# Banded attention on one core: the order of TensorE's products within a step, and where a group's last value products stand

## The chip, the cores and the metric

The kernel runs on one core of one Trainium2 chip. The metric is the device time of one execution in microseconds. Of three runs of the kernel before, the median is 1149.72 us, the lowest 1143.83 us and the highest 1149.92 us.

## The reference

The reference is one decoder-like stack on x of 2 x 1024 x 128 values. Four layers follow one another, each with a layer norm and a residual: full attention over x, a mixture of 64 experts (plus two shared ones), a banded attention with causal window, and the same mixture again. The change touches only the banded attention:

```
q, k, v = heads of (x @ W + b), 16 heads of width 8        # two batches, s = 1024 in the shape used here
valid   = (j <= i) & (j >= i - 32 + 1)
attn    = softmax(where(valid, q @ k.T * 8**-0.5, -inf))
out     = (attn @ v) @ Wo + bo
```

A query sees itself and the 31 keys ahead of it, so of each row of scores only a band is computed: for a tile of 128 queries, 160 keys.

## The kernel before

**Tiling.** `banded_attention` calls `attend_banded` (L534). The 2 batches x 16 heads are cut into 8 groups `n` of 4 heads; each group is walked in 8 steps `s` of 128 keys. The four heads of a group lie in pairs: pair `pr` 0 on partitions 0 to 47, pair 1 on partitions 64 to 111, and `h` picks the head within a pair. I write "step 4.3" for step 3 of group 4.

**One step on TensorE** (`stage`, L706 to L741) issues, in this order:

- the two mask products (L721, whole array, 128 rows by 128 columns, 320 columns of data), one into each bank `st[pr]`. Each first waits for the exponential of the step before on that bank (L720);
- two scores of pair 0 for a later group (`scores`, L658, 48 rows), which wait until VectorE has reduced the tile before them in the bank `sc[0]`. Each later group's maxima are needed before its exponentials, so its scores run four steps ahead;
- the four transposed scores of this group (L728, 51 rows), added onto the mask;
- a slot of side work (`next(beside, None)`);
- two scores of pair 1 (`sc[1]`);
- the value products of the step before (`weigh`, L662; products of 128 rows by 32 columns of the array into the banks `pv`);
- in step 5 the turn of the next group's maxima (`turn_max`), and then a second slot of side work.

After its eighth step the group's last `weigh` follows at once (L741). It waits for the exponentials of step 7.

**The other engines.** ScalarE (L775 to L798) waits for the transposed scores and takes two exponentials a step (L787), the side slots standing behind the first and behind the second; at step 4 and step 7 it copies half of the group's sums out of `pv` (L794) and counts `u_out`. VectorE (L839 to L850) reduces the two banks of scores (L828), with one side slot between the banks and one behind them. GpSimd copies the next values (L612) once `pv_done` shows that the group before has been weighed, and splits the maxima. SyncE loads the stacks.

**Side work.** Groups 0 to 3 are batch 0; beside them runs `second_batch`, the norm and the q, k, v projections of batch 1. Beside groups 4 to 7 runs `first_batch`: output projection tile by tile (`out_by_tiles_tensor`, L1261), norm and routing of batch 0. Each engine has its own generator and takes one piece of it per slot; semaphores tie the pieces together. Two pieces matter below. In `out_by_tiles`, an odd slot on TensorE holds `project(t)` (L1279) and `turn(t + 1)` (L1268), and the next, even one holds `turn_back(t + 1)` (L1275), which waits for `att_ready`, that is for VectorE's `divide(t + 1)` (L1311, L1315), which waits for the turn. `project` waits for ScalarE's copy (L1301), which ScalarE takes behind its first exponential. In `qkv_tensor` (L1620) the third to sixth pieces wait for VectorE's `rest` (L1682), pieces 16 to 19 counted from 0: step 1.0's and step 1.1's.

The mixture's experts (`experts`) follow as a block of their own when the attention's block has ended.

Of the kernel before, what the change touches and what calls it, by code (L numbers as in the profile page):

```python
# [27 lines left out]
TB = S // P  # L28
# [505 lines left out]
def attend_banded(nc, env, tag):  # L534
# [8 lines left out]
    with ExitStack() as ctx:  # L543
# [30 lines left out]
        def score_blocks(s, k, nxt, nxt2):  # L574

            if s < STEPS - AHEAD:
                return [(1, (k + 1) % 3, s + AHEAD)] if nxt else []
            return [(2, (k + 2) % 3, s - (STEPS - AHEAD))] if nxt2 else []

        @block.sync  # L580
# [70 lines left out]
        def _(pe):  # L651
# [10 lines left out]
            def weigh(n, k, s):  # L662

                pe.wait_ge(exp_done, FREE_ST + n * 2 * STEPS + 2 * s + 2)
                if s == 0:
                    pe.wait_ge(u_out, ONE + n * 2)
# [39 lines left out]
            def stage(r, k, nxt, nxt2):  # L706
# [7 lines left out]
                for s in range(STEPS):  # L714
                    width = BAND if s < STEPS - 1 else P
                    if s == STEPS - AHEAD and nxt2:
                        pe.wait_ge(loaded[(k + 2) % 3], (r + (k + 2) // 3) * LOADS + LOADS)
                    for pr in range(2):
                        e = 2 * s + pr
                        pe.wait_ge(exp_done, n * 2 * STEPS + e + 1)  # L720
                        pe.matmul(st[pr][:, :], env.ident16[:, :], mask_k[:, :], start=True, stop=True)  # L721
                    blocks = score_blocks(s, k, nxt, nxt2)
                    for off, kk, qt in blocks:
                        scores(n + off, kk, qt, 0)
# [8 lines left out]
                    next(beside, None)  # L733
                    for off, kk, qt in blocks:
                        scores(n + off, kk, qt, 1)
                    if s:
                        weigh(n, k, s - 1)
                    if s == STEPS - AHEAD + TURN and nxt:
                        turn_max(n + 1)
                    next(beside, None)  # L740
                weigh(n, k, STEPS - 1)  # L741
# [4 lines left out]
        def _(act):  # L746
# [24 lines left out]

            second, first = second_batch(), first_batch()
            copy_max(0)

            def stage(r, k, nxt, nxt2):  # L775
# [4 lines left out]
                for s in range(STEPS):  # L780

                    if s >= 2:
                        act.wait_ge(pv_done, ONE + n * STEPS + s - 1)
# [7 lines left out]
                    if s in (TB // 2, STEPS - 1):  # L791
                        half = 0 if s == TB // 2 else 1
                        act.wait_ge(pv_done, ONE + n * STEPS + TB // 2 * (half + 1))
                        act.copy(env.u[:, bass.ds(n, 1), half * CH:(half + 1) * CH].rearrange("p o c -> p (o c)"),  # L794
                                 pv[half][:, :]).then_inc(u_out, 1)
# [1315 lines left out]
```

## Time and profile before

| | |
|---|---|
| median of 3 runs | 1149.72 us |
| lowest, highest | 1143.83, 1149.92 us |
| span of the profiled execution | 1143.3 us |
| loop of the banded attention, first mask product to the experts' first product | 726.6 to 861.0 us |
| TensorE, VectorE, ScalarE, GpSimd busy over the span | 91%, 81%, 62%, 40% |

The profiled execution has no time of its own beside its span; the span lies 0.5 us under the lowest run, and 6.4 us under the median. A profile lists instructions with start and duration on each engine; a line like L721 is a line of the kernel before. TensorE's products are pipelined: one that lasts 0.23 us may start 0.08 us after the one ahead of it, so for TensorE the starts tell more than the durations. "Idle before" names what the engine had last waited for.

### The profile page before, as it was taken

The page shows a single profiled execution, that of the slowest core. Times are in us where ns is not written, and L with a number is a line of the kernel's source. Part 1 is how long each engine was busy: PE and PEld are TensorE (multiplying, and loading weights), DVE is VectorE, ACT ScalarE, POOL GpSimd, SP SyncE. Part 2 cuts the span into 40 slices and gives each one's busy share as a digit, 9 for nine tenths or more (in the row PEclk, how much of TensorE's full clock was granted, in tenths as well). Part 3 has the DMA queues.
Part 4 walks back from the last instruction along what each step waited for, and adds up shares of the span by engine and source line. Part 5 has one row for each costly group of instructions (what it writes and reads, how often), then busy time and mean ns, then how long its engine had stood idle before and what let it go on. Part 6 is the DMA issues. An engine that isn't in the chain of part 4 may idle for free. (4 is left out here: it accounts for less than half of the span.)

```text
span 1143.3 us, 18866 instructions
## 1 busy us (share of the span) xinstructions
PE 1044.1 (91%) x6314; PEld 427.5 (37%) x6314; DVE 925.3 (81%) x2139; ACT 709.0 (62%) x1089; POOL 461.7 (40%) x434
## 2 busy tenths in 40 slices
PE   5769999999999979999999998888888999999998
PEld 4212222222222325444444443334444444444443
DVE  8688999999998467889788776877876779877775
ACT  2537778777787765666666664355465566666664
POOL 4116336532100105565564554100113556556554
PEclk9758999999999989999999999679999999999999
DMA  6901302311200126566764873142206667687662
GB/s 207 253 2 28 81 9 72 80 53 28 54 2 1 43 59 170 163 170 174 196 181 140 218 193 81 34 110 59 72 4 172 157 152 188 171 208 193 182 189 57
DMA packets 72185, 131.63 MB, mean 115 GB/s; under 512 B 12680, under 2 KB 47624, under 8 KB 72088
## 3 DMA queue, kind: packets, MB, share of 16 engines
q1 hardware_dynamic: 68704, 120.92, 40.5%
q10 hardware_dynamic: 3384, 9.51, 3.1%
q8 instruction: 50, 0.82, 0.3%
q14 instruction: 47, 0.39, 0.1%
HBM read 115.08 MB, written 14.91 MB: 114 GB/s over the span
## 5 line engine op out<-in xcount | busy, mean ns | idle before, releaser
L421 ACT ACTIVATE Aatt_prob<-Aatt_st 128x1024 f32<-128x1024 f32 x256 | 247.7, 1022 | 66.1 <-PE Aatt_st L315 65.1
L487 DVE TENSOR_REDUCE Aatt_mx<-Aatt_sc 128x1 f32<-128x512 f32 x439 | 273.3, 683 | 10.0 <-PE Aatt_sc L302 9.5
L1993 POOL TENSOR_TENSOR M1ex_low<-M1ex_hid,M1ex_high 128x512 f16<-128x512 f32 x132 | 152.8, 1157 | 136.2 <-ACT M1ex_high L1892 70.1
L1993 POOL TENSOR_TENSOR M2ex_low<-M2ex_hid,M2ex_high 128x512 f16<-128x512 f32 x132 | 152.7, 1157 | 130.8 <-PE M2ex_acc L1848 73.3
L302 PE MATMUL Aatt_sc<-ks,qs 48*128 48x512 bf16 x496 | 152.5, 408 | 29.5 <-DVE Aatt_mx L487 11.8
L1886 ACT ACTIVATE M2ex_sil<-M2ex_ring,unscale 128x512 f32<-128x512 f32 x132 | 90.7, 687 | 95.3 <-PE M2ex_ring L1831 95.1
L1886 ACT ACTIVATE M1ex_sil<-M1ex_ring,unscale 128x512 f32<-128x512 f32 x132 | 90.7, 687 | 89.4 <-PE M1ex_ring L1831 88.9
L327 PE MATMUL Aatt_pv<-Aatt_prob,vg 128*32 128x512 f32 x1024 | 137.9, 611 | 0.6 <-ACT Aatt_prob L421 0.6
L1930 DVE SCALAR_TENSOR_TENSOR M2ex_ring<-M2ex_ring,unscale,M2ex_sil 128x512 f32<-128x512 f32 x132 | 100.0, 757 | 42.0 <-ACT M2ex_sil L1886 38.9
L1930 DVE SCALAR_TENSOR_TENSOR M1ex_ring<-M1ex_ring,unscale,M1ex_sil 128x512 f32<-128x512 f32 x132 | 99.9, 757 | 36.2 <-ACT M1ex_sil L1886 32.9
L302 PEld LDWEIGHTS Aatt_sc<-ks,qs 48*128 48x128 bf16 x496 | 35.9, 94 | 201.1 <-DVE Aatt_mx L487 167.7
L315 PE MATMUL Aatt_st<-qs,ks 51*128 51x512 bf16 x512 | 105.2, 387 | 4.0 <-ACT Aatt_prob L421 2.6
L1940 DVE TENSOR_TENSOR M1ex_hid<-M1ex_ring,M1ex_cb 128x512 f32<-128x512 f32 x132 | 91.3, 692 | 16.2 <-DVE M1ex_ring L1930 0.9
L1940 DVE TENSOR_TENSOR M2ex_hid<-M2ex_ring,M2ex_cb 128x512 f32<-128x512 f32 x132 | 91.3, 692 | 15.9 <-DVE M2ex_ring L1930 0.5
L828 DVE CUSTOM_DVE_ANT_0 Batt_sc<-Batt_sc,mask 128x160 f32<-128x160 f32 (+1 forms) x256 | 75.2, 347 | 25.5 <-PE Batt_sc L658 24.1
L1892 ACT CAST M1ex_high<-M1ex_hid 128x512 f16<-128x512 f32 x132 | 80.6, 610 | 17.9 <-DVE M1ex_hid L1940 15.9
L1892 ACT CAST M2ex_high<-M2ex_hid 128x512 f16<-128x512 f32 x132 | 80.5, 610 | 12.1 <-DVE M2ex_hid L1940 10.4
L787 ACT ACTIVATE Batt_prob<-Batt_st 128x320 f32<-128x320 f32 x128 | 51.1, 436 | 55.3 <-PE Batt_st L728 54.9
L1829 PE MATMUL M1ex_ring<-M_xh,M_wt 128*128 128x512 f16 x132 | 50.5, 383 | 11.0 <-DVE M1ex_hid L1940 5.4
L248 POOL CAST Aatt_mparts<-Aatt_m 128x32 bf16<-128x32 f32 x8 | 2.6, 325 | 140.1 <-DVE Aatt_m L500 140.1
L1829 PE MATMUL M2ex_ring<-M_xh,M_wt 128*128 128x512 f16 x132 | 50.4, 382 | 5.7 <-DVE M2ex_hid L1940 3.4
L1848 PE MATMUL M2ex_acc<-M2ex_low,M_wt 128*128 128x512 f16 x132 | 50.3, 381 | 1.0 <-POOL M2ex_low L1993 1.0
(437 smaller groups left out, 1959.5 us busy)
## 6 DMA issues: line engine op xcount, KB each, us to landing
M1ex_cb<-comb SPq DMA_DIRECT2D x130, 256.0 KB, 4.1
M2ex_cb<-comb SPq DMA_DIRECT2D x130, 256.0 KB, 4.2
M_wt<-wsplit SPq DMA_DIRECT2D x132, 192.0 KB, 4.0
wsplit<-split_cut SPq DMA_DIRECT2D x9, 704.0 KB, 4.5
qs<-stack SPq DMA_DIRECT2D x32, 96.0 KB
ks<-stack SPq DMA_DIRECT2D x30, 96.0 KB
split_raw<-in_wg_dram ACTq DMA_DIRECT2D x3, 704.0 KB, 8.5
split_raw<-in_wu_dram ACTq DMA_DIRECT2D x3, 704.0 KB, 12.0
```

The source lines that it names most:

```text
L302: mm = pe.matmul(sc_bank(n, i), queries, ks[k][rows, jp, h * CH:(h + 1) * CH], start=True, stop=kind != "excess")
L315: mm = pe.matmul(st[jp][:, half, :], ks[k][rows, jp, kc * P:(kc + 1) * P], qs[k][rows, jp, qh * CH:(qh + 1) * CH], start=True, stop=True)
L327: mm = pe.matmul(pv[32 * j:32 * j + 32, :], vg[k][:, kc, j, :], prob[(2 * s + j % PAIR) % 4][:, j // PAIR, :], start=kc == 0, stop=kc == T ...
L421: act.activation(prob[e % 4][:, :, :].rearrange("p a c -> p (a c)"), st[pr][:, :, :].rearrange("p a c -> p (a c)"), ACT.Exp, scale=SCALE). ...
L487: ins = dve.tensor_reduce(mx[k][:, m, h:h + 1], scores, AX.X, ALU.max)
L828: ins = dve.tensor_tensor_reduce(scores, scores, mask_q[:, first:BAND], -1.0, -BARRED, ALU.add, ALU.min, accum_out=m1[k][:, j, qt:qt + 1])
L1829: pe.matmul(gate(q)[:, :], wt[k][:, 0, :], env.xh[:, cs], start=True, stop=False)
L1886: act.activation(sil[q % 2][:, :], gate(q)[:, :], ACT.Silu, scale=env.unscale[:, 0:1]).then_inc(sil_ready, 1)
L1892: act.copy(high[q % 3][:, :], hid[q % 3][:, :]).then_inc(high_ready, 1)
L1930: dve.scalar_tensor_tensor(up(q)[:, :], up(q)[:, :], env.unscale[:, 1:2], sil[q % 2][:, :], ALU.mult, ALU.mult).then_inc(up_ready, 1)
L1940: dve.tensor_tensor(hid[q % 3][:, :], up(q)[:, :], cb[k][:, c * CH:(c + 1) * CH], ALU.mult).then_inc(hid_ready, 1)
L1993: pool.tensor_tensor(low[q % 3][:, :], hid[q % 3][:, :], high[q % 3][:, :], ALU.subtract).then_inc(low_ready, 1)
```

## The change

Within a step, TensorE's work is put in the order of its tiling: whole-array products first (the side slots and the masks), then all 64-row products (transposed scores, then both pairs' scores), then the 32-column value products. The two side slots move: the slot that stood last in a step now stands ahead of the next step's first mask product (the same place in the stream), and the slot that stood behind the transposed scores now stands between the two mask products. The first slot of groups 0 and 4 is left out on TensorE, which keeps the numbering of the slots against ScalarE and VectorE. Scores of pair 0 no longer stand ahead of the transposed scores.

Between groups of one batch (`carried`), the last `weigh` of a group moves behind the first transposed scores and scores of the next group. ScalarE's copy of the second half of the sums moves behind the two exponentials of the next group's step 0, and the waits on `u_out` are split by half.

```diff
+        def carried(n):
+            return n % G < G - 1
@@ TensorE, weigh
-                if s == 0:
-                    pe.wait_ge(u_out, ONE + n * 2)
+                if s == 0 and n:
+                    pe.wait_ge(u_out, ONE + 2 * n - 1)
+                if s == 3:
+                    pe.wait_ge(u_out, ONE + 2 * n)
@@ TensorE, stage
                     for pr in range(2):
+                        if pr or s or n % G:
+                            next(beside, None)
                         e = 2 * s + pr
                         pe.wait_ge(exp_done, n * 2 * STEPS + e + 1)
                         pe.matmul(st[pr][:, :], env.ident16[:, :], mask_k[:, :], start=True, stop=True)
-                    blocks = score_blocks(s, k, nxt, nxt2)
-                    for off, kk, qt in blocks:
-                        scores(n + off, kk, qt, 0)
                     for h in range(2):
                         for pr in range(2):
 ...
-                    next(beside, None)
-                    for off, kk, qt in blocks:
-                        scores(n + off, kk, qt, 1)
+                    for off, kk, qt in score_blocks(s, k, nxt, nxt2):
+                        for pr in range(2):
+                            scores(n + off, kk, qt, pr)
                     if s:
                         weigh(n, k, s - 1)
+                    elif n and carried(n - 1):
+                        weigh(n - 1, (k + 2) % 3, STEPS - 1)
                     if s == STEPS - AHEAD + TURN and nxt:
                         turn_max(n + 1)
-                    next(beside, None)
-                weigh(n, k, STEPS - 1)
+                if not carried(n):
+                    weigh(n, k, STEPS - 1)
@@ ScalarE, stage
-                    if s >= 2:
+                    if s:
                         act.wait_ge(pv_done, ONE + n * STEPS + s - 1)
 ...
-                    if s in (TB // 2, STEPS - 1):
-                        half = 0 if s == TB // 2 else 1
-                        act.wait_ge(pv_done, ONE + n * STEPS + TB // 2 * (half + 1))
-                        act.copy(...).then_inc(u_out, 1)
+                    if s == 0 and n and carried(n - 1):
+                        sums_out(n - 1, 1)
+                    if s == TB // 2:
+                        sums_out(n, 0)
+                    if s == STEPS - 1 and not carried(n):
+                        sums_out(n, 1)
```

`sums_out(n, half)` is the wait and the copy that stood there before. No product, exponential or reduction is added or dropped.

## Rows read from the trace of the kernel before

**Rows 1.** The page: span, and TensorE's granted clock in 40 slices, tenths of full.
```profile
span 1143.3 us, 18866 instructions
PEclk9758999999999989999999999679999999999999
```

**Rows 2.** Busy time by stretch: us, each engine's busy us, PEclk, DMA share, GB/s.
```profile
726.60:738.30 11.70, 11.18 (x110) 5.07 (x109) 10.61 (x73) 4.81 (x13) 2.55 (x5) 0.54 0.18 46
738.30:756.60 18.30, 16.25 (x142) 7.98 (x143) 14.88 (x67) 11.44 (x25) 0.40 (x1) 1.00 0.27 68
756.60:772.80 16.20, 15.05 (x158) 6.28 (x154) 9.72 (x65) 7.42 (x19) 1.30 (x5) 0.58 0.49 125
...
794.00:816.60 22.60, 21.11 (x220) 12.84 (x221) 18.32 (x95) 10.00 (x29) 1.31 (x5) 1.00 0.33 96
```

**Rows 3.** Timeline of TensorE, step 3.6, no side work: start us, length us, what.
```profile
789.35 0.64 PE L721 MATMUL Batt_st<-mask,ident 128*128 128x320 bf16 x2
789.92 0.24 PE L658 MATMUL Batt_sc<-ks,qs 48*128 48x160 bf16 x1
...
790.14 0.23 PE L728 MATMUL Batt_st<-qs,ks 51*128 51x160 bf16 x1
...
790.96 0.31 PE L721 MATMUL Batt_st<-mask,ident 128*128 128x320 bf16 x1 [0.17 <-ACT Batt_prob L787]
```

**Rows 4.** Timeline of ScalarE in that same step.
```profile
790.47 0.77 ACT L787 ACTIVATE Batt_prob<-Batt_st 128x320 f32<-128x320 f32 x2 [0.70 <-PE Batt_st L728]
```

**Rows 5.** Timeline of TensorE, step 7.5, which has no scores.
```profile
853.15 0.64 PE L721 MATMUL Batt_st<-mask,ident 128*128 128x320 bf16 x2 [0.17 <-ACT Batt_prob L787]
...
854.62 0.64 PE L721 MATMUL Batt_st<-mask,ident 128*128 128x320 bf16 x2 [0.18 <-ACT Batt_prob L787]
```

**Rows 6.** Timeline of TensorE from step 2.7 to step 3.1, over a group's end.
```profile
777.49 0.64 PE L721 MATMUL Batt_st<-mask,ident 128*128 128x320 bf16 x2 [0.17 <-ACT Batt_prob L787]
...
779.40 0.43 PE L671 MATMUL Batt_pv<-Batt_prob,vg 128*32 128x128 f32 x8 [0.50 <-ACT Batt_prob L787]
...
781.11 0.64 PE L721 MATMUL Batt_st<-mask,ident 128*128 128x320 bf16 x2 [0.52 <-ACT Batt_prob L787]
```

**Rows 7.** Timeline of TensorE, step 0.2, at half clock.
```profile
730.53 0.71 PE L721 MATMUL Batt_st<-mask,ident 128*128 128x320 bf16 x2
...
732.52 0.45 PE L721 MATMUL Batt_st<-mask,ident 128*128 128x320 bf16 x1
```

**Rows 8.** Timeline of TensorE beside the output projection: turn 1, step 4.5, turn 7.
```profile
797.67 0.60 PE L1268 MATMUL Batt_side<-ident,u 128*128 128x128 f32 x4
...
806.05 0.60 PE L1268 MATMUL Batt_side<-ident,u 128*128 128x128 f32 x4
806.49 0.43 PE L721 MATMUL Batt_st<-mask,ident 128*128 128x320 bf16 x2
...
806.95 0.36 PE L728 MATMUL Batt_st<-qs,ks 51*128 51x160 bf16 x3
807.40 0.33 PE L1275 MATMUL Batt_side<-ident,Batto_att 128*128 128x128 f32 x1
...
808.68 0.60 PE L1268 MATMUL Batt_side<-ident,u 128*128 128x128 f32 x4
...
813.85 0.60 PE L1268 MATMUL Batt_side<-ident,u 128*128 128x128 f32 x4
```

**Rows 9.** Timeline of ScalarE in step 4.5.
```profile
807.40 0.44 ACT L787 ACTIVATE Batt_prob<-Batt_st 128x320 f32<-128x320 f32 x1 [0.95 <-PE Batt_st L728]
807.77 0.27 ACT L1301 COPY Batto_attT<-Batt_side 128x128 f32<-128x128 f32 x1
```

**Rows 10.** Timeline of VectorE in step 4.5.
```profile
807.05 0.29 DVE L1315 TENSOR_TENSOR Batto_att<-Batt_side,Batto_rden 128x128 f32<-128x128 f32 x1
```

**Rows 11.** Timeline of TensorE, step 1.1, beside the projections.
```profile
749.38 1.16 PE L1634 MATMUL Batt_side<-b_wv,Battqln_xnT 128*128 128x128 f32 x8 [0.35 <-DVE Battqkv_rest L1682]
```

**Rows 12.** Timeline of VectorE in step 1.1.
```profile
750.37 0.74 DVE L1682 SCALAR_TENSOR_TENSOR Battqkv_rest<-Batt_side,b_bqk,Battqkv_part 128x512 f32<-128x512 f32 x1
```

More of the change, by code:

```diff
@@ L770, in first_batch, with sums_out @@
                 yield from route_scalar(act, env, n1, q1, bank, 0)
+            def sums_out(n, half):
+                act.wait_ge(pv_done, ONE + n * STEPS + TB // 2 * (half + 1))
+                act.copy(env.u[:, bass.ds(n, 1), half * CH:(half + 1) * CH].rearrange("p o c -> p (o c)"),
+                         pv[half][:, :]).then_inc(u_out, 1)
             second, first = second_batch(), first_batch()
@@ L790, in stage @@
                             next(beside, None)
-                    if s in (TB // 2, STEPS - 1):
-                        half = 0 if s == TB // 2 else 1
-                        act.wait_ge(pv_done, ONE + n * STEPS + TB // 2 * (half + 1))
-                        act.copy(env.u[:, bass.ds(n, 1), half * CH:(half + 1) * CH].rearrange("p o c -> p (o c)"),
-                                 pv[half][:, :]).then_inc(u_out, 1)
+                    if s == 0 and n and carried(n - 1):
[4 more added lines that the diff above has]
+                        sums_out(n, 1)
                     if s == STEPS - AHEAD + TURN and nxt:
```

## The prediction, made before the changed kernel ran

> **What bounds the kernel now.** I first took the page for the span and the clock [rows 1], then cut the banded loop into stretches [rows 2], then read single steps in the timeline of TensorE and set those of ScalarE and VectorE beside them. The loop fills 726.6 to 861.0 us, 134.4 us for 64 steps, mean 2.1 us; everything else in the program is untouched and follows it in series, so what the loop gains or loses the span gains or loses. The busy shares mislead here: TensorE is busy 16.3 of 18.3 us in the stretch with the projections [rows 2], yet what sets a step differs by kind of step.
>
> *Steps without side work at full clock.* A ring of two engines. Step 3.6 starts its first mask at 789.35 and step 3.7 at 790.96, 1.61 us later, and that mask had waited for an exponential [rows 3]. Round the ring: second mask (0.64 - 0.31 = 0.33 after the first, so 789.68) to the first 64-row product at 789.92 is 0.24; the last transposed product starts 0.22 later at 790.14 and lasts 0.23; the exponentials start at 790.47 and take 0.77 together [rows 3, 4]; then the next second mask. Sum 0.24 + 0.22 + 0.23 + 0.10 + 0.77 + 0.05 = 1.61. VectorE is not in this ring.
>
> *Steps at half clock.* The granted clock reads 0.54 and 0.58 in two stretches, that is mostly 1.2 GHz [rows 2]; 13 steps lie there, and one takes 1.99 us [rows 7].
>
> *Steps beside the output projection* (4.1 to 5.0). TensorE and a chain through VectorE and ScalarE. One period, turn to turn, is 808.68 - 806.05 = 2.63 us [rows 8].
>
> *Steps beside the projections* (0.7 to 1.4). VectorE, with 14.9 busy of 18.3 us [rows 2]; TensorE stood 0.35 us for VectorE's `rest` before the even slot of step 1.1 [rows 11].
>
> **The change part by part.**
>
> *Transposed scores first.* Pair 0's scores leave the ring. The trace shows what the ring is without them: from step 7.5 to 7.6, where no scores remain, 854.62 - 853.15 = 1.47 us [rows 5], against 1.61 [rows 3]: 0.14 a step. The scores then run beside the exponentials, where TensorE had 0.17 us idle before the mask [rows 3]. VectorE gets them some 0.15 us later; it has room where no side work runs. Steps of this kind: 8 clean ones in groups 2 and 3, and six in groups 5 and 6 where VectorE also carries side work, counted at half: 8 x 0.14 + 6 x 0.07 = 1.5 us. Bounds 0 and 14 x 0.14 = 2.0. At half clock TensorE itself nearly fills the step, for the first mask came without a wait [rows 7]; I take 0.07, half the above, for 13 steps: 0.9 us, bounds 0 and 13 x 0.28 = 3.6 (the full-clock gap doubled). Together 2.4.
>
> *Last value products carried over.* At a group's end `weigh` stands 0.50 us for the exponentials, and the next step's second one is short because both masks are free. Two steps over the end of group 2 take 781.11 - 777.49 = 3.62 us against 2 x 1.61 = 3.22 in the middle of a group [rows 3, 6]: 0.40 us a boundary. Once carried, the products lie beside the exponentials. ScalarE's copy of 0.58 us moves into step 0 of the next group, behind the exponentials; ScalarE waits 0.70 us for TensorE in a step [rows 4], so it is covered; were it not, it would cost what is over. GpSimd's copy of the next values comes one step later and is wanted only a group later; nothing else is queued there but the splitting of maxima, which waits for VectorE. There are six carried boundaries; two of them (0 to 1, 4 to 5) lie in the chains below. Four times 0.40, with 0.2 more for the one at half clock: 1.8 us; bounds 0.8 and 2.4.
>
> *Fewer changes of tiling.* A side slot behind the transposed scores cuts the 64-row products in two. In step 4.5 the last of these starts at 806.95 + 0.36 - 0.23 = 807.08 and the side product at 807.40; in an unbroken run they follow each other every 0.07 us ((0.36 - 0.23) / 2). Some of the 0.32 is waiting for VectorE, which ended at 807.34 [rows 8, 10], so the change of tiling itself is bounded by 0.24 us from above and by 0 from below; I take 0.09, twice a step. Further, pair 0's and pair 1's products run side by side when nothing stands between, and two of the six start places fall away: 0.15. Together 0.3 us in a step with side work in its even slot and no chain. Those are 5.7, 6.1 and 7.6: 0.9 us.
>
> The Trainium skill ("TensorEngine Tiling (Array Packing)", section Tiling Modes) says that a change of tiling mode, not of tile, drains the engine. The rows do not separate a drain from a wait here. By that rule alone, with the bound of 0.24 us from the rows for each and 16 steps losing two changes, the loop would win 7.7 us; this is a rival below.
>
> *The even slot between the masks: the output projection.* Here the cover goes. Before, `turn_back` came 0.3 us behind the last transposed product: the masks and the 64-row products (806.49 to 807.31) hid VectorE's `divide`. Now only one mask stands between `turn` and `turn_back`. From the last turn's start (806.05 + 0.60 - 0.27 = 806.38) to `turn_back`'s start at 807.40 is 1.02 us, and VectorE ended 0.06 before it [rows 8, 10]; those 1.02 us are latency and remain. Behind the waiting `turn_back` stand the second mask, the transposed scores, and so the exponentials. Then: `turn_back` to second mask 0.17 (half of its 0.33), to the transposed scores 0.24, their second start and length 0.31, to the exponential 0.09: it starts at 1.83. ScalarE's copy starts 0.37 behind it and takes 0.27 [rows 9], so `project` may start at 2.51, and from `project` to the last turn is 0.60. Period 3.11 us against 2.63. TensorE's own work would have let `project` start at about 2.15, so the copy is late by a further 0.36; both waits are in the 3.11. The six periods from turn 1 to turn 7 took 813.85 - 797.67 = 16.2 us before [rows 8]; now 6 x 3.11 = 18.7: +2.5. The step after turn 7 pays another 0.6 and the boundary gives 0.3 back: +2.8 us in all, bounds +1.0 (if only the first wait bit) and +4.5.
>
> *The same slot beside the projections.* The `rest` that lets a piece go is taken by VectorE behind the first bank of that step's scores. These now stand behind the even slot, which holds TensorE for 1.1 us or more (1.16 for the values [rows 11]). So the odd piece's `rest` comes about as much later. In step 1.0 about half of that had been lost before in other work; in step 1.1 piece 18 stands for `rest` (0.74 us [rows 12]) and piece 19's `rest` can't begin before it is through. Worked through by these durations step 1.1 starts 0.8 us later and step 1.2 starts 2.2 us later, the gain at the boundary 0 to 1 included. VectorE is the bound up to step 1.4, so nothing of it comes back: +2.2 us, bounds 0 and +3.6.
>
> *Sum.* -2.4 - 1.8 - 0.9 + 2.8 + 2.2 = -0.1 us. Against the profiled execution, 1143.3 us becomes 1143.2 us. The median of the runs lies 6.4 us above that span, and I leave that distance as it is: 1149.7 - 0.1, rounded to 1149.6 us.
>
> **The rivals.**
>
> *A. The waits are covered and the drains count.* If VectorE and ScalarE run ahead in the side chains, the losses vanish, and every one of 16 steps with even side work wins 0.3: -2.4 - 1.8 - 16 x 0.3 = -9.0, time 1140.7 us. For it: TensorE is the busiest engine in the loop. Against it: the 1.02 us of latency stand in the rows. The rule of the skill in its strongest form comes to -2.4 - 1.8 - 7.7 = -11.9, 1137.8 us.
>
> *B. The clock.* The two half-clock stretches end sooner because steps are denser. A step takes 1.99 at half and 1.61 at full clock [rows 3, 7]: 13 x 0.38 = 4.9 us, time 1144.7 us. For it: the work per time rises. Against: TensorE was busy 11.2 of 11.7 us there and stayed at half [rows 2].
>
> *C. Slower.* The idle time that the even slot now opens in steps 4.1 to 5.0, some 1.2 us of a period of 3.11, lets TensorE's granted clock fall there to half. Per step the 0.38 above and as much again for the side products: 8 x 0.8 = +6.4, time 1156.0 us. It decides from the point where the stage's clock, 1.00 before [rows 2], falls below about 0.6. Against it: the ring steps at 1.61 us have as large a share of waiting and keep the full clock.
>
> *D. It doesn't do what it says.* The array runs the two pairs in its own order and the transposed scores come no sooner: the 2.4 and 0.9 go, +5.0 - 1.8 = +3.2, time 1152.9 us. Against it: rows 5.
>
> **How the numbers follow.** Chances: forecast 0.48, A 0.19, B 0.10, C 0.13, D 0.10. A measurement of this kernel tells apart about 0.5%, 5.7 us. A lies beyond that, B just inside; of the forecast, with unknowns of some 4 us both ways, a tenth falls out on each side. Faster 0.19 + 0.03 + 0.05 = 0.27; slower 0.13 + 0.01 + 0.05 = 0.19; same 0.54. The forecast's own range is 1144 to 1155; with half of A and C it is 1141 to 1156.
>
> **What would show it.** In the changed profile: ring steps in groups 2 and 3 at 1.47 us (transposed first); no 0.5 us wait before the 128-column value products except after groups 3 and 7 (carried); turn to turn 3.1 us in group 4, with TensorE's L1275 waiting some 0.8 us each for `att` and `project` some 0.3 us for `attT`; step 1.2 starting 2 us later after step 0.7 than before. The prediction is wrong if turn to turn stays near 2.6, or if the clock row of the loop differs from the one before by more than a slice.

## The result, and the profile after

The changed kernel took 1154.81 us, the median of 20 runs, against 1149.70 us for the kernel before, the median of 20 runs on the same chip: a ratio of 1.0054, 95% interval 1.0033 to 1.0076. Ratios, means and half-clock times here and below leave out runs more than 1.5% above the fastest of their kernel; medians are of all runs. The forecast was 1149.6 us, a change of -0.1 us, with "same" as the likeliest case. The time lies just inside the range given, at its upper end, which is no merit of the sum: the median rose by 5.1 us where almost nothing was forecast.

The profiled execution took 1152.56 us with a span of 1150.8 us, 7.5 us more than the span before [rows 1]. The page of the changed kernel, its span and its clock row:

```profile
span 1150.8 us, 18881 instructions
...
PEclk9758999999999989999999998689969999999999
```

The clock row shows the first surprise: besides the 6 and 8 of slices 26 and 27, where 6 and 7 stood before [rows 1], there is a second 6 in slice 30, about 834 to 863 us. A piece of the loop that ran at full clock before now runs at half, from 833.3 to 853.8 us. ("Half clock" is a granted clock of 0.50, the lower of the two levels.)

The loop, from its first mask to the experts' first product, is the stretch 726.6 to 861.0 us before and 726.8 to 870.4 us after. Each row is: stretch, us, busy us of TensorE, its weight loads, VectorE, ScalarE and GpSimd, the granted clock, DMA share, GB/s. Before:

```profile
726.60:861.00 134.40, 116.62 (x1296) 57.07 (x1295) 100.52 (x561) 70.67 (x177) 15.52 (x39) 0.91 0.22 59
```

After:

```profile
726.80:870.40 143.60, 120.00 (x1296) 58.90 (x1296) 98.86 (x561) 70.00 (x177) 15.57 (x39) 0.85 0.20 55
```

The same numbers of instructions take 9.2 us longer; the rest of the program is 1.7 us shorter (behind the loop it has one stretch of 3.4 us at half clock where the kernel before has two), which leaves the 7.5 us. Now the same view cut at the same steps. Before, steps 1.2 to 3.7, 4.0 to 5.0, 5.1 to 5.7, and 6.0 to 6.7 are the stretches from 752.2, 794.1, 816.6 and 831.3 us; the last three:

```profile
794.10:816.60 22.50, 21.05 (x220) 12.75 (x221) 18.32 (x95) 10.00 (x29) 1.31 (x5) 1.00 0.33 96
816.60:831.30 14.70, 12.06 (x154) 5.83 (x152) 12.92 (x87) 6.80 (x17) 2.50 (x5) 1.00 0.17 40
831.30:846.10 14.80, 12.79 (x157) 6.50 (x153) 11.73 (x60) 9.34 (x23) 3.66 (x7) 1.00 0.01 3
```

After, steps 1.2 to 3.7 and those three:

```profile
754.50:794.00 39.50, 35.03 (x434) 16.28 (x432) 28.61 (x180) 20.95 (x53) 3.94 (x15) 0.87 0.34 88
794.00:820.50 26.50, 19.40 (x219) 11.38 (x220) 17.01 (x93) 8.88 (x29) 1.20 (x5) 1.00 0.30 88
820.50:835.70 15.20, 12.31 (x145) 6.03 (x144) 13.04 (x89) 7.16 (x18) 2.62 (x6) 0.92 0.10 23
835.70:855.00 19.30, 18.62 (x156) 9.18 (x153) 12.75 (x67) 9.46 (x23) 3.66 (x7) 0.53 0.01 3
```

| stretch | before, us | after, us | difference | forecast |
|---|---|---|---|---|
| steps 0.0 to 1.1 | 25.6 | 27.7 | +2.1 | +1.8 |
| steps 1.2 to 3.7 | 41.9 | 39.5 | -2.4 | about -2.6 |
| steps 4.0 to 5.0 | 22.5 | 26.5 | +4.0 | +2.8 |
| steps 5.1 to 5.7 | 14.7 | 15.2 | +0.5 | steps 5.1 to 7.7: |
| steps 6.0 to 6.7 | 14.8 | 19.3 | +4.5 | about -2.1 |
| steps 7.0 to 7.7 | 14.9 | 15.4 | +0.5 | |

The forecast column spreads the terms of the sum over their steps. The first two rows came out near the forecast, the second of them in part by the clock, as is shown below; the rest did not.

*The ring, as forecast.* TensorE in the changed kernel, the masks of steps 2.5, 2.6 and (behind them) 2.7:

```profile
775.19 0.64 PE L730 MATMUL Batt_st<-mask,ident 128*128 128x320 bf16 x2
775.76 0.31 PE L735 MATMUL Batt_st<-qs,ks 51*128 51x160 bf16 x4
775.91 0.42 PE L662 MATMUL Batt_sc<-ks,qs 48*128 48x160 bf16 x4
...
776.76 0.53 PE L730 MATMUL Batt_st<-mask,ident 128*128 128x320 bf16 x2
```

The transposed products (L735) lead, the scores (L662) follow 0.15 us behind. Step 2.5 takes 776.76 - 775.19 = 1.57 us and step 2.6 takes 778.18 - 776.76 = 1.42, mean 1.50, where 1.61 stood before [rows 3] and 1.47 was forecast. Not every such step is shorter: step 3.3 went from 1.70 to 2.21 us, because the mask of step 3.4 waits for a stack that is being loaded, a wait that the kernel before does not have:

```profile
786.82 0.45 PE L730 MATMUL Batt_st<-mask,ident 128*128 128x320 bf16 x2 [0.67 <-DMA ks<-stack]
```

*The boundary, half given back.* TensorE over the end of group 2, to be set beside rows 6:

```profile
778.18 0.58 PE L730 MATMUL Batt_st<-mask,ident 128*128 128x320 bf16 x2
...
779.24 0.48 PE L677 MATMUL Batt_pv<-Batt_prob,vg 128*32 128x160 f32 x8
...
780.39 0.45 PE L730 MATMUL Batt_st<-mask,ident 128*128 128x320 bf16 x2 [0.67 <-DMA qs<-Batt_mt]
...
781.15 0.42 PE L677 MATMUL Batt_pv<-Batt_prob,vg 128*32 128x128 f32 x8
...
781.61 0.31 PE L730 MATMUL Batt_st<-mask,ident 128*128 128x320 bf16 x1
```

The 128-column value products of the old group (781.15) stand behind the new group's first scores and no longer wait 0.50 us for exponentials: the carrying over does what it says. But the new group's first mask waits 0.67 us for something that was never late before: the group's maxima, which a transfer brings into the query rows (`qs<-Batt_mt`, issued at 777.31). From step 2.7 to step 3.1 is 781.61 - 778.18 = 3.43 us, against 3.62 before [rows 6] and 2 x 1.47 = 2.94 forecast.

*Beside the output projection, as forecast.* TensorE in step 4.5, to be set beside rows 8:

```profile
808.07 0.60 PE L1284 MATMUL Batt_side<-ident,u 128*128 128x128 f32 x4
808.50 0.30 PE L730 MATMUL Batt_st<-mask,ident 128*128 128x320 bf16 x1
809.41 0.33 PE L1291 MATMUL Batt_side<-ident,Batto_att 128*128 128x128 f32 x1 [0.61 <-DVE Batto_att L1331]
809.58 0.30 PE L730 MATMUL Batt_st<-mask,ident 128*128 128x320 bf16 x1
809.81 0.31 PE L735 MATMUL Batt_st<-qs,ks 51*128 51x160 bf16 x4
...
811.19 0.60 PE L1284 MATMUL Batt_side<-ident,u 128*128 128x128 f32 x4
```

One mask stands between `turn` (L1284) and `turn_back` (L1291), which waits 0.61 us for VectorE; the second mask and all 64-row products stand behind it. Turn to turn is 811.19 - 808.07 = 3.12 us; 3.11 was forecast. ScalarE, in the same step, stands 1.71 us for the transposed scores, against 0.95 before [rows 9]:

```profile
810.22 0.44 ACT L802 ACTIVATE Batt_prob<-Batt_st 128x320 f32<-128x320 f32 x1 [1.71 <-PE Batt_st L735]
```

What TensorE waited for in the whole stretch 794.0 to 820.5 us of the changed kernel (what waits, for whom, us in total, times, longest), of which the kernel before had 0.7 us once and 0.2 us once:

```profile
PE Batt_side L1291 <- DVE Batto_att L1331: 5.2, 8, 1.1
PE Batt_side L1295 <- ACT Batto_attT L1317: 1.5, 7, 0.3
```

### The profile page after: what moved, and what is told of

Same layout as the page of the kernel before. It is cut to its first block and busy times, and to the rows that moved or that the text cites. A ratio compares the mean times of both kernels' runs of the same rounds, so it can differ in the third digit from the quotient of the medians.

```text
span 1150.8 us, 18881 instructions
## 1 busy us (share of the span) xinstructions
PE 1046.9 (91%) x6314; PEld 429.4 (37%) x6314; DVE 923.2 (80%) x2139; ACT 709.1 (62%) x1089; POOL 462.2 (40%) x434
## 5 line engine op out<-in xcount | busy, mean ns | idle before, releaser
L2009 POOL TENSOR_TENSOR M1ex_low<-M1ex_hid,M1ex_high 128x512 f16<-128x512 f32 x132 | 152.9, 1158 | 136.1 <-ACT M1ex_high L1908 70.1
```

What stands on the lines that cost most here:

```text
L2009: pool.tensor_tensor(low[q % 3][:, :], hid[q % 3][:, :], high[q % 3][:, :], ALU.subtract).then_inc(low_ready, 1)
```

## The experiments

The rival theories at this point: W, the added time is waiting that the new place of the even slot causes, to be had back by moving the slot; C, it is the half-clock time that the changed kernel has more of. (The expectations use these letters, and others that they explain.) Runs of one kernel scatter (the changed one: 1152.3 to 1165.0 us), and each run lists its mean granted clock, from which twice the missing share times the run's time is the time spent at half clock. Over all runs here, time rises by 0.28 us for each us of it, within a kernel. So each result below has three numbers: the median with the ratio to the kernel before, the mean time with the mean half-clock time, and the mean moved by that slope to 119 us of half clock, called the levelled time. The kernel before, over its 96 runs: mean 1149.7, half clock 129.0, levelled 1146.9 (error 0.2). The changed one: 1155.8, 142.8, 1149.1 (error 0.35). The runs below were taken in three sittings, each on a chip of its own, and the kernel before differed between them: mean 1147.9 with 123.0 us of half clock beside the first four experiments, 1149.6 with 128.9 beside the four with the slot behind scores or a mask twice, 1151.9 with 136.1 beside the order alone and the three with ring masks. A difference of a few us of half clock between kernels of different sittings therefore shows nothing. The levelled time leans on the slope, and a later section says where that fails.

**The last value products alone.** The kernel before, with only the carrying over (the waits and the place of `weigh`; ScalarE's copy moves as in the change):

```
-                if s == 0:
-                    pe.wait_ge(u_out, ONE + n * 2)
+                if s == 0 and n:
+                    pe.wait_ge(u_out, ONE + 2 * n - 1)
+                if s == 3:
+                    pe.wait_ge(u_out, ONE + 2 * n)
...
+                    elif n and carried(n - 1):
+                        weigh(n - 1, (k + 2) % 3, STEPS - 1)
```

> The kernel before with one part of the change alone: the last value products of groups 0, 1, 2, 4, 5 and 6, and the copy of their second half, move into the next group's step 0; the order within a step is as before. Theory W (waits at the even side slot between the masks cost the time): this part wins what I forecast for it, 0.4 us at each of five or six boundaries, so 1.8 to 2.4 us, ratio to before 0.998. Rival K (carrying the products over costs, because ScalarE's copy or GpSimd's copy of the next values comes late): 2 us or more slower, ratio 1.002 or above. Rival C (only the granted clock of the loop decides): time by its half-clock stretches, no step changed but those at the boundaries.

Measured: 1152.6 us, ratio 1.0027 (0.9996 to 1.0058); mean 1151.2 with 141.0 us of half clock, levelled 1145.1 (error 0.7), which is 1.8 below the kernel before; 1.8 was forecast. The plain ratio, 0.998 expected, is above 1 instead: the kernel has 18 us more of half clock than the kernel before in its sitting. Its TensorE over the end of group 2, at full clock:

```profile
777.76 0.64 PE L727 MATMUL Batt_st<-mask,ident 128*128 128x320 bf16 x2 [0.17 <-ACT Batt_prob L801]
...
779.65 0.45 PE L727 MATMUL Batt_st<-mask,ident 128*128 128x320 bf16 x2 [0.48 <-ACT Batt_prob L801]
...
781.01 0.64 PE L727 MATMUL Batt_st<-mask,ident 128*128 128x320 bf16 x2 [0.16 <-ACT Batt_prob L801]
```

Two steps take 781.01 - 777.76 = 3.25 us against 3.62 [rows 6]: 0.37 gained, 0.40 forecast, and nobody waits for the maxima. So at this boundary the wait of 0.67 us comes from the two parts together: with the transposed scores first as well, TensorE reaches the boundary sooner than the transfer lands. (The order alone, below, waits 0.44 and 0.75 us for the maxima at the ends of groups 1 and 3, and not here.)

**The even slot back behind the transposed scores.** The changed kernel with the slot between masks moved (here and below, conditions that are always true or false are left out of the code shown):

```
                     for pr in range(2):
-                        if pr or s or n % G:
+                        if not pr and (s or n % G):
                             next(beside, None)
...
+                    next(beside, None)
                     for off, kk, qt in score_blocks(s, k, nxt, nxt2):
```

> The changed kernel with the even side slot put back behind the transposed scores (before the scores of both pairs) in all groups; everything else as changed. Theory W: the losses of the changed kernel vanish (4.0 us in steps 4.0 to 5.0, 2.2 in 0.0 to 1.1, some 5 in 5.7 to 6.7) and the gains stay: 4 to 6 us faster than before, ratio 0.995 to 0.997; turn to turn in group 4 back to 2.6 us. Rival C (the order itself thins TensorE's work so that the clock falls to half in groups 5 and 6, wherever the slot stands): that stretch of 20 us remains, ratio 1.000 or above.

Measured: 1149.23 us, 1.0018 (0.9998 to 1.0039); mean 1149.5 with 130.3, levelled 1146.3. A gain of 4 to 6 us on the kernel before was expected; it did not come. Turn to turn was 2.6 us again, so the group 4 loss is the slot's. But steps 1.0 and 1.1 stayed at 4.45 and 5.13 us (before 3.17 and 4.16; changed 4.73 and 5.40). VectorE and TensorE of this kernel in step 1.0:

```profile
747.28 0.33 DVE L846 CUSTOM_DVE_ANT_0 Batt_sc<-Batt_sc,mask 128x160 f32<-128x160 f32 x1 [1.52 <-PE Batt_sc L662]
```

```profile
745.90 1.10 PE L1646 MATMUL Batt_side<-Battqln_xnT,b_wqk 128*128 128x512 f32 x2
...
748.70 1.10 PE L1646 MATMUL Batt_side<-Battqln_xnT,b_wqk 128*128 128x512 f32 x2 [1.10 <-DVE Battqkv_rest L1700]
```

VectorE stands 1.52 us for scores that are queued behind the projection product at 745.90, and then TensorE stands 1.10 us for VectorE's `rest`. The two wait for each other in turn. It is not enough that the slot leaves the masks; it has to be behind the scores.

**The slot back in group 4 only, and from step 5.1 on only.**

```
-                        if pr or s or n % G:
+                        if (pr and not (n in (4, 5) and n * STEPS + s <= 5 * STEPS)) or (not pr and (s or n % G)):
...
+                    if n in (4, 5) and n * STEPS + s <= 5 * STEPS:
+                        next(beside, None)
```

> The changed kernel with the even side slot behind the transposed scores only from step 4.0 to step 5.0 (the output projection). Theory W: turn to turn 2.6 us there, 4.0 us less than the changed kernel, ratio to before 1.002; the half-clock stretch of groups 5 and 6 stays. Rival C: if the half-clock stretch follows from the thin steps of group 4, it goes as well, and the ratio is 0.997.

Measured: 1151.14 us, 1.0020 (0.9997 to 1.0043); 1150.3 with 134.8, levelled 1145.8: 3.3 less than the changed kernel, where 2.5 to 2.8 was the forecast's price of that chain and +4.0 is what the stretch showed. Steps 4.5 to 4.7 take 2.63, 2.59 and 2.60 us again. Its profiled execution also speaks on the clock:

```profile
PEclk8758999999998999999999998688979999999999
...
790.00:816.00 26.00, 24.04 (x216) 13.11 (x213) 16.28 (x90) 10.24 (x29) 1.30 (x5) 0.74 0.11 33
```

The half-clock stretch in group 6 is still there (17.1 us from 835.2, the 7 in slice 30), although group 4 has its old slots; and 13.7 us of half clock now lie in group 4 itself, from 797.7. So, as far as one execution shows it, the stretch in group 6 does not need the waits of group 4.

The second kernel has `n * STEPS + s > 5 * STEPS` in both places:

> The changed kernel with the even side slot behind the transposed scores only from step 5.1 on (norm and routing). Theory W with the clock as its consequence: without the waits of steps 5.7 to 6.2 the half-clock stretch does not come, 4 to 6 us less than the changed kernel, ratio to before 1.000 to 1.002. Rival C (the fall to half clock does not depend on the slot here): the stretch stays, at most 2 us less, ratio 1.004.

Measured: 1152.83 us, 1.0039 (1.0018 to 1.0061); 1152.5 with 131.4, levelled 1149.0. That is the changed kernel's 1149.1: by this measure the place of the slot costs and brings nothing from step 5.1 on, though the mean time is 3.3 us lower, with 11 us less of half clock. Of the 4 to 6 us expected, 3.3 came, and only together with the clock: in its profiled execution 6.8 us of half clock are left in group 6, where the changed kernel has 20.5.

**The slot behind both scores**, ahead of the value products, in all groups:

```
                     for off, kk, qt in score_blocks(s, k, nxt, nxt2):
                         for pr in range(2):
                             scores(n + off, kk, qt, pr)
+                    next(beside, None)
```

> The changed kernel with the even side slot behind the scores of both pairs and ahead of the value products, in all groups. Theory W, second half (in groups 0 and 1 the loss comes from the scores standing behind the slot, not from the slot standing between the masks): steps 1.0 and 1.1, 4.45 and 5.13 us with the slot behind the transposed scores and 4.73 and 5.40 in the changed kernel, return to 3.2 and 4.2 us; at equal half-clock time 2 us less than with the slot behind the transposed scores and 4.5 to 5 us less than the changed kernel, so some 2.5 us faster than before. Rival S (VectorE is bound there for another reason, the later start of the scores within the step): they stay above 4.2 and 4.9. Half-clock time, which by the runs so far costs 0.28 us for each us: between that of before (mean 124 us) and of the changed kernel (143), so the plain ratio lies between 0.998 and 1.003.

Measured: 1146.06 us, 0.9973 (0.9943 to 1.0002); 1147.0 with 137.5, levelled 1141.8, that is 7.3 below the changed kernel and 5.1 below the one before. TensorE of this kernel in a step of group 4:

```profile
803.72 0.43 PE L730 MATMUL Batt_st<-mask,ident 128*128 128x320 bf16 x2
...
804.63 0.33 PE L1293 MATMUL Batt_side<-ident,Batto_att 128*128 128x128 f32 x1
...
805.66 0.60 PE L1286 MATMUL Batt_side<-ident,u 128*128 128x128 f32 x4
806.10 0.43 PE L730 MATMUL Batt_st<-mask,ident 128*128 128x320 bf16 x2
```

No row of the step has a wait, and it takes 806.10 - 803.72 = 2.38 us, against 2.63 before [rows 8] and 3.12 in the changed kernel. Steps 1.0 and 1.1 take 3.21 and 4.24 us, as in the kernel before.

**The same in groups 0 and 1 only**, the slot elsewhere as in the changed kernel (condition `n < 2`):

> The changed kernel with the even side slot behind both pairs' scores in groups 0 and 1 alone (the projections). Theory W: steps 1.0 and 1.1 take 3.2 and 4.2 us, 2.2 to 2.8 us less than the changed kernel at equal half-clock time; groups 4 to 7 keep turn to turn at 3.12 us. Rival S: they stay above 4.2 and 4.9 us and the time at equal half-clock time is that of the changed kernel.

Measured: 1153.55 us, 1.0027 (0.9995 to 1.0059); 1153.6 with 142.3, levelled 1147.0: 2.1 less than the changed kernel at the same half-clock time, so here the slope plays no part. The forecast's term for this chain was +2.2. Steps 1.0 and 1.1: 3.21 and 4.25 us.

**The order alone**, without the carrying over (`carried` returns False and the old wait stands):

> The changed kernel without the carrying over: each group's last value products and the copy of its second half stand where they stood before; the order within the step is the changed one. Theory W: at equal half-clock time 1.9 us more than the changed kernel and 4.2 us more than before (the waits of groups 1 and 4, 5.4 us, less about 1 us for the earlier transposed scores). Whether the carrying over is what adds half-clock time is open (that part alone had a mean of 148 us of it, before 128, the changed kernel 143): if so, this kernel has 125 to 130 us and a plain ratio of 1.004; if it is the order, 140 us or more and a ratio of 1.006 to 1.008.

Measured: 1158.79 us, 1.0046 (1.0016 to 1.0076); 1158.3 with 143.6, levelled 1151.4: 2.3 above the changed kernel, which gives the carrying over its price a second time, and 4.5 above the kernel before. At full clock the price shows at the ends of groups 4 and 6 (step 4.7 takes 3.79 us against 3.15 in the changed kernel, step 6.7 2.13 against 1.84), and not at the end of group 2 (3.34 us for steps 2.7 and 3.0 against 3.43), where the changed kernel waits for the maxima. Which part brings the half-clock time is not settled: against the kernel before in the same sitting the carrying over alone has 18 us more (error 5.5), this kernel 7.5 (error 5), and both parts with the slot behind the transposed scores 7 (error 3).

**More work for TensorE.** If the granted clock follows how densely TensorE works (theory G in the expectations), products that do nothing new, put where it waits, should cut the half-clock time. Pair 0's mask is written twice in every step, which leaves the result as it was; in the changed kernel, and in the one with the slot behind both scores:

```
-                        pe.matmul(st[pr][:, :], env.ident16[:, :], mask_k[:, :], start=True, stop=True)
+                        for _ in range(2 - pr):
+                            pe.matmul(st[pr][:, :], env.ident16[:, :], mask_k[:, :], start=True, stop=True)
```

> The changed kernel with each step's first mask product made twice into the same bank. Between the masks of the changed kernel TensorE waits in the side steps (0.9 us each in group 4), so the extra product is covered there too. Theory G: the half-clock stretch of some 20 us in groups 5 and 6 becomes rare, half-clock time falls from 143 to 125 us or less, and the plain ratio to before falls from 1.0054 to 1.002 or less. Rival N: the half-clock time stays at 140 us and the ratio rises to 1.006 by the added products.

Measured: 1152.36 us, 1.0006 (0.9983 to 1.0028); 1152.0 with 112.7 us of half clock, where the changed kernel has 142.8.

> As the kernel with the slot behind both pairs' scores, and each step's first mask product is made twice into the same bank. In steps without side work TensorE has idle time between its two masks, so the extra 0.14 us costs nothing there; in some 20 steps in which TensorE is full it costs 0.14 to 0.27 us, 3 to 4 us in all. Theory G (the granted clock follows how much TensorE does, and the changed kernel's plain time suffers from more half-clock time): half-clock time falls below that of before, to 110 us or less, which is worth 5 us or more against the changed kernel's 143; plain ratio to before 0.998 to 1.002. Rival N (half-clock time is chance or has another cause): it stays between 125 and 145 us and the ratio is 1.003 or more.

Measured: 1147.54 us, 0.9963 (0.9932 to 0.9994); 1147.1 with 114.1, from 137.5. In both the half-clock time falls by 23 to 30 us, while the mean time falls by 3.8 us in the first and not at all in the second: in steps without a wait ahead of the masks the added product costs its 0.13 us.

**The second mask only in the ring steps**, where the mask stands waiting anyway: `range(2 if pr == 0 and ring(n, s) else 1)`, with `ring` true in steps 1.2 to 3.7, 5.1 to 5.7 and 6.2 to 7.7. In the changed kernel, in the one before, and with the slot behind both scores:

> The changed kernel with the first mask product made twice, but only in steps 1.2 to 3.7, 5.1 to 5.7 and 6.2 to 7.7, where TensorE waits for the exponentials between its masks; the steps beside the projections and the output projection, and those of group 0, are as changed. Theory G (the granted clock follows TensorE's work per time): half-clock time falls from 143 to 125 us or less with at most 1 us of added work, so the plain ratio to before falls from 1.0054 to 1.000 to 1.003. Rival N (the earlier fall in half-clock time came from group 0, where masks twice ended its half-clock stretch 3.4 us sooner): half-clock time stays above 135 us, ratio 1.005.

Measured: 1153.44 us, 1.0014 (0.9981 to 1.0047); 1153.6 with 119.2. The half-clock stretch of 20.5 us in group 6 is down to 3.4 in the profiled execution, from 836.3 us, most of which lies in this row:

```profile
837.00:852.00 15.00, 13.73 (x167) 7.43 (x164) 11.28 (x65) 9.02 (x23) 2.90 (x7) 0.91 0.01 2
```

Steps 6.0 and 6.1 take 2.08 and 2.10 us here, 3.67 and 3.61 in the changed kernel at half clock, 2.20 and 2.55 in the kernel before.

> The kernel before with the first mask product made twice in the same steps (1.2 to 3.7, 5.1 to 5.7, 6.2 to 7.7). Theory G: half-clock time, 128 us on average before, falls to 120 us or less; at 0.28 us for each that is 2 to 3 us faster, ratio 0.998, and fewer runs above 1155 us. If the added product is not covered in the order of before, it costs 0.14 us in some 35 steps, up to 5 us, and the ratio is 1.002.

Measured: 1148.76 us, 0.9957 (0.9931 to 0.9984); 1148.7 with 118.7. This kernel and the last have the same half-clock time and differ by the change alone: 4.9 us by their means. Their profiles differ by stretch, in the order of the table above, by +2.1, -1.2, +4.0, +0.8, about 0 and +0.6 us, together +6.2 where the means say 4.9.

> The slot behind both pairs' scores, with the first mask product made twice in the same steps. Mechanically 5 us less than before (as measured at equal half-clock time for the slot behind the scores), at most 1 us for the added products; half-clock time 120 us or less by theory G instead of 137. Expected 1140 to 1143 us, ratio to before 0.993 to 0.996, the fastest of all. Rival N: half-clock time stays at 137 us, ratio 0.998.

Measured: 1143.87 us, ratio 0.9911 (0.9875 to 0.9947); 1144.0 with 110.5. It beats the changed kernel and the one before. Its page and its loop:

```profile
span 1142.6 us, 18967 instructions
...
PEclk9758999999999999999999999599999999999999
```

```profile
726.80:860.20 133.40, 117.64 (x1342) 58.92 (x1342) 103.19 (x583) 70.85 (x176) 15.58 (x39) 0.92 0.22 60
```

The doubled masks add TensorE work (117.64 us busy, 116.62 before) and next to no time to the ring: steps 3.0 and 7.0, which have no wait to hide them, take 0.13 us more. The waits for transfers are still in it, and longer: the masks wait 4.7 us in all, five times, three for the maxima and two for a stack (1.23 and 1.53 us). The kernel before has none. One of them, at the end of group 2:

```profile
782.33 0.58 PE L734 MATMUL Batt_st<-mask,ident 128*128 128x320 bf16 x3 [0.56 <-DMA qs<-Batt_mt]
```

## Why the prediction was wrong, step by step

The -0.1 us was a small difference of larger terms. The pair with ring masks, at equal clock, shows +6.2 us in its profiles. The step that failed is the gains, which were mis-sized: steps 1.2 to 3.7 gave -1.2 us where -2.6 was forecast, and steps 5.1 to 7.7 gave +1.2 where -2.1 was forecast (transposed scores first in groups 5 and 6 and at half clock, fewer changes of tiling, two carried boundaries). Together that is 4.7 us. The loss beside the output projection was mis-sized by a further 1.2 us (+4.0 for +2.8). And the sum had no term for the clock. Term by term:

*Transposed scores first, full clock (-1.5).* Mechanism right, and the size too in steps 2.5 and 2.6: 1.50 us a step, 1.47 forecast. Over a whole group it brought less, since TensorE now also runs ahead of transfers: steps 3.0 to 3.6 take 10.71 us against 11.21 before, half of the forecast 0.14 a step, with the wait of 0.67 us for the stack in them; the kernel with the order alone, which has no such wait there, takes 10.09. The six steps counted at half in groups 5 and 6 are the mis-sized part, and the pair with ring masks shows them at equal clock (kernel before first): steps 5.2, 5.4 and 5.5 take 1.66, 1.52 and 1.61 us, then 1.88, 1.69 and 1.60, while step 5.3 falls from 2.19 to 1.82, so that steps 5.1 to 5.5 are 0.1 us shorter in all; steps 6.4, 6.5 and 6.6 take 1.41, 1.47 and 1.47 us in both. The latter stood at the ring without scores all along: group 6 has no later group left to score in them, which the trace before would have told. In group 5, where VectorE carries side work, its scores are probably what comes late; whether the 0.15 us by which they stand further back is the whole of it was not measured.

*The same at half clock (-0.9).* Failed. Steps 0.2 to 0.4, at half clock, take 1.99, 2.06 and 1.92 us before, 1.99, 2.00 and 1.93 after. TensorE fills such a step [rows 7], and its products in another order are not fewer.

*Carrying over (-1.8).* Right by itself: -1.8 levelled, 0.37 us at the boundary that was looked at. Only half right in company: the boundary of the changed kernel has 0.19 us less than before, for the mask then waits for the maxima's transfer. The prediction named what moves behind the exponentials on ScalarE and GpSimd, and left out who else must be ready for the new group's first step.

*Fewer changes of tiling (-0.9).* Seen in the steps, not in the sum. At full clock step 6.1 went from 2.55 to 2.10 us and step 7.6 from 2.25 to 2.07 (changed kernel: 1.93), where 0.3 each was forecast; step 5.7 can't be read, since part of it lies in half clock. But the neighbours took it back: 6.2 and 6.3 are longer by 0.24 and 0.28, 7.3 by 0.28, 7.7 by 0.42. From step 5.1 to the end the pair shows +1.2 us where about -2.1 was forecast, and the kernel that puts the slot of these groups back is as fast as the changed one (levelled 1149.0 and 1149.1). A step that ends sooner only meets VectorE's chain sooner. The stronger rule, that a change of tiling mode drains the engine (the Trainium skill, "TensorEngine Tiling (Array Packing)", Tiling Modes), is not refuted by this; its price was not to be had back here.

*The even slot beside the output projection (+2.8).* The period was right to 0.01 us and its six repeats too: steps 4.2 to 4.7 are longer by 2.6 us, 2.5 forecast. The ends were mis-sized. Step 4.1, where the first `turn_back` waits, pays 0.53 that was not counted, and step 5.0 takes 2.62 us against 1.83, 0.79 more, where 0.6 less 0.3 for the boundary was put. Sum +4.0; 3.3 come back when the slot is put back.

*The slot beside the projections (+2.2).* Right: the loop is 2.1 us late at step 1.2 in the profile, and 2.1 us come back when the slot of groups 0 and 1 goes behind the scores. The reason was right as well: the prediction put it in the scores that stand behind the even slot. With the slot behind the transposed scores, where it no longer stops the masks but the scores still stand behind it, the steps stayed nearly as long (4.45 and 5.13 us); with the slot behind the scores they fell to 3.21 and 4.24.

*The clock.* The sum had no term for it, and rival C put the loss in steps 4.1 to 5.0. These kept the clock at 1.00; the new half-clock stretch of 20.5 us (833.3 to 853.8) came in steps 5.7 to 6.7 instead. The prediction named "more than a slice" in the clock row as a sign that it was wrong, and this is what happened. TensorE was busy 19.40 of 26.50 us in group 4 ahead of it (0.73), against 21.05 of 22.50 (0.94) before. That looks like the cause and is not shown to be: with group 4's slots put back the stretch stays (17.1 us), and the order alone, as thin in group 4, has only 3.4 us there. What the profiles do show is that it shrinks to 6.8 us with the slots of groups 5 to 7 put back and to 3.4 with them all put back. That half-clock time goes with the amount of TensorE's work is borne out by the doubled masks, which add to that work and little else and take 23 to 30 us of half clock away. Part of the clock came as a gift too: the first stretch of half clock behind step 1.2 lasted 10.2 us in place of 13.7, which is why steps 1.2 to 3.7 show -2.4 us here and only -1.2 in the pair with ring masks.

*The rivals.* A fell with the waits of 5.2 and 1.5 us, D with the ring at 1.50, B in the main: only one of the stretches ended sooner, by 3.5 us, and a longer one opened. C was right in kind and wrong in place, and its reason, the idle time in steps 4.1 to 5.0, is not borne out.

*What stays open.* How the 6.1 us between the means split. By the slope of 0.28 us, 13.8 us of half clock are 3.9 us, and 2.2 are left for the waits. By the pair with equal half clock the waits are 4.9 us, and little is left for the clock. The slope holds between runs of one kernel; from kernel to kernel the ring masks took 10 to 27 us of half clock away and 1.0 to 3.0 us of time, about 0.1 us per us (17 us and 3.2 us, 0.2, for the kernel before against the runs of its own sitting). Half-clock time costs most where TensorE bounds the step (steps 6.0 and 6.1: 1.6 and 1.5 us each) and least where a step is bound by others. The sum of both is settled, the share is between 2 and 5 us for the waits. It is not known either what places a fall: the changed kernel has one in group 6 and none in group 4, while the kernel with group 4's slots put back has one in each (13.7 us from 797.7, 17.1 us from 835.2). The runs show only that half-clock time goes down with added work. And each stretch is known from one execution of its kernel.

## What to carry to other kernels

Order TensorE's products by tiling mode only if none of those brought forward waits for a result that another engine has just begun: where engines hand work round, who stands behind a side piece decides its place, and the place behind all that others wait for (0.9973, 0.9943 to 1.0002) beat the place that saved mode changes (1.0054, 1.0033 to 1.0076). When a wait at a boundary is removed, ask what else must be there for the next group, its transfers above all. And look at the granted clock after every change in the order of work: half-clock time can appear in steps that were not touched, and work that costs nothing, put into a wait, can win some back (0.9911 together with the better place of the slot).

## What the runs showed of the hardware

Added TensorE work made a kernel faster. With the first mask written twice in 43 ring steps, the kernel before went to 0.9957 (0.9931 to 0.9984) of its own time in the same sitting, its half-clock time from 136 us to 119, and its ring steps stayed as long as they were, but for those without a wait, such as steps 3.0 and 7.0, 0.13 us longer. In all five kernels with doubled masks the half-clock time fell.

The scatter of one kernel's runs is in good part the clock's: the changed kernel's twenty runs lie between 1152.3 and 1165.0 us, and time goes with half-clock time at 0.28 us per us. A mean clock, listed with each run, told kernels apart that medians alone did not.

Products of 64 rows in opposite halves of the array run side by side where they follow each other in the program: in the carrying over alone, pair 0's scores start at 776.72 us and pair 1's transposed product at 776.73, each 0.24 us long:

```profile
776.72 0.24 PE L662 MATMUL Batt_sc<-ks,qs 48*128 48x160 bf16 x1
776.73 0.24 PE L734 MATMUL Batt_st<-qs,ks 51*128 51x160 bf16 x1
```
